# Attention front of a one-core transformer layer: six output slots for values, the first queries and keys in halves, plain scores one tile sooner

## The chip, the cores and the metric

The kernel runs on one core of a Trainium2 chip. The metric is device time in microseconds (us). The engines are TensorE (PE in the profile, its weight loads PEld), VectorE (DVE), ScalarE (ACT), GpSimd (POOL) and SyncE (SP), which here issues all DMA transfers on one queue.

## What is computed

A layer on 2048 tokens of width 512: a normalisation, causal attention with 16 heads of 32, and a gated feed-forward part with a hidden width of 4096.

```python
xn = layernorm(x)
qkv = xn @ w_qkv.T                       # 3 x 16 heads x 32
scores = q @ k.T / sqrt(32)              # causal: only keys up to the query
attn = softmax(scores) @ v
gate, up = xn @ Wg.T, xn @ Wu.T
out = x + attn @ w_o.T + (gelu(gate) * up) @ Wd.T
```

All of it is float32; the kernel splits an operand in a high and a low part and multiplies in three passes where one pass is too coarse.

## The kernel before

Three blocks follow each other: `norm_and_project`, `attention`, `project_and_feed_forward`. Within a block each engine runs its own list of instructions, in the order in which the program issues them, and waits on semaphores; there is no planner.

`norm_and_project` makes the normalised tokens and the queries and keys, which it stores to `qk_scratch` in memory, and the values of the first two tiles of 128 tokens (`V_FIRST`), left in PSUM in `p_v`.

`attention` begins with the *value stage*. TensorE makes the values of tiles 2 to 15, twelve matmuls each (`values`, lines 49 to 51 in `mm3`), in turn in three PSUM banks, `bank_st` (`p_v` twice and `p_st3`, `ST_BUFS` = 3). It makes tile v when ScalarE has placed tile v - 3. ScalarE's `value_out(v)` (lines 727 to 735) waits for the tile, waits for the slot, copies the tile to one of two slots in `o_sb` (line 731), and copies its heads of the first two pairs to `v_stack` (line 733). SP then stores the slot to `v_scratch` in memory (line 540).

```python
            if v >= 2:
                act.wait_ge(v_stored[v % 2], 16 * (v // 2))
```

The attention goes by eight pairs of heads. A pair needs its queries and keys in `q_stack` and `k_stack`: `load_head` (lines 517 to 523) issues six DMAs of 32 rows by 2048 columns, 256 KB each, for each of its two heads. SP's order in the value stage is: head 0 of pair 0, store 0, head 1, stores 1 to 8, head 0 of pair 1, stores 9 and 10, head 1 of pair 1, stores 11 to 15.

*Units* are plain score tiles (queries in rows), at most 512 keys wide, `scores(n)`, line 855; VectorE takes their row maxima, with a mask on the diagonal (line 767) or without (line 771). They use four banks `p_s` in turn, so unit n waits for the maximum of unit n - 4 (`bank_free`). A pair has 80 units. 44 of pair 0 are put behind value tiles 6 to 14: four behind tile 6, five behind each other (`BEHIND_V`, `FIRST_V`). The LEAD stage behind tile 15 has the next eight units and the first eight *transposed scores* (`scores_t`, line 883), whose exps ScalarE makes (line 708) and GpSimd sums (line 635). Then the main loop runs 80 groups: a group has eight transposed scores, its units, four products with the values (line 909) and row sums (line 923). The units run ahead of what needs them by a fixed number: `unit_end` says how many are done after each group, 12 in the first, then 8 in each until all 640 are made. The row maxima are split by GpSimd (lines 650 to 658) and turned into rows by TensorE (line 865).

On the first use of a pair (units 0 and 1) TensorE waits for `qk_loaded`. Later pairs are loaded by SP in the middle of the pair before.

Of the kernel before, what the change touches and what calls it, by code (L numbers as in the profile page):

```python
# [20 lines left out]
F32 = mybir.dt.float32  # L21
# [5 lines left out]
ACT = mybir.ActivationFunctionType  # L27
# [3 lines left out]
S = 2048  # L31
H = 512
NH = 16
D = H // NH
MLP = 4096
KT = H // P
TT = S // P
W = 512
TC = S // W
# [272 lines left out]
def attention(nc, qk_scratch, v_scratch, sum_scratch, rsum_scratch, wo_t, wo_sb, attn_t, xn_hi, xn_lo, e_sb, wv_hi, wv_lo, p_v,  # L312
# [5 lines left out]
    PB = 2  # L318
# [10 lines left out]
    UNITS_FIRST = (20, 12)  # L329
    UNITS_AHEAD = 56  # L330
    TURN_LEAD = 1


    STEPS = [(qc, kt, max(0, kt * P - qc * W)) for qc in range(TC) for kt in range(4 * qc + 4)]
# [11 lines left out]
    NU = len(UNITS)  # L346
    UNITS_TO = [sum(1 for a, i, b, w in UNITS if i < 4 * r + 4) for r in range(TC)]
    NUNIT = PAIRS * NU
    MASKED_UNITS = [n for n in range(NUNIT) if UNITS[n % NU][2] == UNITS[n % NU][1] // 4]

    BEHIND_V = {v: 4 if v == 6 else 5 for v in range(6, TT - 1)}
    FIRST_V = sum(BEHIND_V.values())
    FIRST = FIRST_V + LEAD * 2
    unit_end, done = [], FIRST
# [58 lines left out]
    with ExitStack() as ctx:  # L415
# [3 lines left out]
        def sem(name):  # L419
            return ctx.enter_context(nc.semaphore(name))  # L420

        q_stack = [[sb(f"q_stack{i}{a}", [P, S], F32R) for a in range(2)] for i in range(PB)]
        k_stack = [[sb(f"k_stack{i}{a}", [P, S], F32R) for a in range(2)] for i in range(PB)]
# [4 lines left out]
        o_sb = sb("o_sb", [P, 2, 2, HALF], F32)  # L428
        rsum_rows = sb("rsum_rows", [P, S], F32)
# [15 lines left out]
        p_o = ctx.enter_context(nc.psum_tensor("p_o", [P, 2, HALF], F32))  # L445

        v_out = sem("v_out")
        v_stored = [sem(f"v_stored{i}") for i in range(2)]
        v_placed = [sem(f"v_placed{i}") for i in range(PB)]
        consts = sem("consts")  # L450
        filled = sem("filled")
        o_cleared = sem("o_cleared")
        qk_loaded = [[sem(f"qk_loaded{i}{a}") for a in range(2)] for i in range(PB)]
        v_loaded = [sem(f"v_loaded{i}") for i in range(PB)]
        scored = sem("scored")
        maxed = sem("maxed")
# [26 lines left out]
        def bank_st(x):  # L483
            return p_v[:, x % ST_BUFS, :] if x % ST_BUFS < V_FIRST else p_st3[:, :]
# [25 lines left out]
        def pooled_to(k, i):  # L510
            return max(count for j in range(i + 1) for vector, count in [made[k, j]] if not vector)

        def attn_rows(p, a, qc):
            cols = slice((p // 2) * S + qc * W, (p // 2) * S + (qc + 1) * W)
            return attn_t[(2 * (p % 2) + a) * D:(2 * (p % 2) + a + 1) * D, cols]

        def load_head(sp, p, a):
            rows = slice((2 * p + a) * D, (2 * p + a + 1) * D)
            for strip, (q_part, k_part) in enumerate(((0, 0), (0, 1), (1, 0))):
                to = slice(strip * D, (strip + 1) * D)  # L520
                sp.dma_start(q_stack[p % PB][a][to, :].bitcast(F32),
                             qk_scratch[0, q_part, rows, :]).then_inc(qk_loaded[p % PB][a], 16)
                sp.dma_start(k_stack[p % PB][a][to, :].bitcast(F32),
                             qk_scratch[1, k_part, rows, :]).then_inc(qk_loaded[p % PB][a], 16)

        def load_v(sp, p):
            sp.dma_start(v_stack[p % PB][:, :, :, :],
# [2 lines left out]

        @block.sync
        def _(sp):
            load_head(sp, 0, 0)
            for v in range(TT):
                if v == 1:
                    load_head(sp, 0, 1)
                if v in (9, 11):
                    load_head(sp, 1, v // 11)
                sp.wait_ge(v_out, v + 1)
                sp.dma_start(v_scratch[v * P:(v + 1) * P, :, :],  # L540
                             o_sb[:, v % 2, :, :].rearrange("p b (h d) -> p (b h) d", d=D)).then_inc(v_stored[v % 2], 16)
            sp.dma_start(wo_sb[:, :, :], wo_t.rearrange("(k p) o -> p k o", p=P)).then_inc(wo_loaded, 16)

            def store_chunk(p, qc):
                c = p * TC + qc
                sp.wait_ge(o_copied, c + 1)
                for a in range(2):
                    for h in range(2):
                        rows = (2 * a + h) * D
                        sp.dma_start(attn_rows(p, a, qc)[:, h * HALF:(h + 1) * HALF],  # L550
                                     o_sb[rows:rows + D, c % 2, 0, :]).then_inc(o_stored[c % 2], 16)
                        first = qc * W + h * HALF
                        sp.dma_start(sum_scratch[2 * p + a:2 * p + a + 1, first:first + HALF],
                                     o_sb[rows:rows + 1, c % 2, 1, :]).then_inc(o_stored[c % 2], 16)

            def load_sums(p):
                for stored in o_stored:
                    sp.wait_ge(stored, 128 * (p + 1) * (TC // 2))
                if p:
                    sp.wait_ge(sums_inverted, p)  # L560
                sp.dma_start(compact[:, :], sum_scratch[2 * p:2 * p + 2, :].rearrange("h (a b) -> (h a) b", b=2 * S // P)
                             ).then_inc(sums_loaded, 16)

            def load_reciprocals(p):
                sp.wait_ge(sums_inverted, p + 1)
                sp.dma_start(rsum_scratch[2 * p:2 * p + 2, :].rearrange("h (a b) -> (h a) b", b=2 * S // P),
                             rcompact[:, :]).then_inc(rsums_out, 16)
                sp.wait_ge(rsums_out, 16 * (p + 1))
                if p >= 2:
                    sp.wait_ge(normalised, TC * (p - 1))  # L570
                for a in range(2):
                    rows = (2 * (p % 2) + a) * D
                    sp.dma_start(rsum_rows[rows:rows + D, :],
                                 rsum_scratch[2 * p + a, :].partition_broadcast(D)).then_inc(rows_loaded, 16)

            for p in range(PAIRS):
                if 0 < p < PAIRS - 1:
                    sp.wait_ge(st_ready, p * NS * PIECES)
                    for a in range(2):
                        load_head(sp, p + 1, a)  # L580
                    sp.wait_ge(pv_done, p * NS)
                    for stored in v_stored:
                        sp.wait_ge(stored, 16 * (TT // 2))
                    load_v(sp, p + 1)
                if p > 0:
                    store_chunk(p - 1, TC - 1)
                    load_sums(p - 1)
                if p < PAIRS - 1:
                    store_chunk(p, 0)
                if p > 0:  # L590
                    load_reciprocals(p - 1)
                if p < PAIRS - 1:
                    for qc in range(1, TC - 1):
                        store_chunk(p, qc)
            sp.wait_ge(wo_loaded, 16)
# [91 lines left out]
        def _(act):  # L687
# [23 lines left out]
            def copy_out(p, qc):  # L711
                c = p * TC + qc
                act.wait_ge(rows_done, (p * NS + CHUNK_START[qc]) // GS + qc + 1)
                if c < 2:
                    act.wait_ge(v_stored[c], 16 * (TT // 2))
                elif p == PAIRS - 1 and qc == 2:
                    act.wait_ge(divided, 4)
                else:
                    act.wait_ge(o_stored[c % 2], 128 * (c // 2))
                nc.scalar.activation(o_sb[:, c % 2, :, :], p_o[:, :, :], ACT.Copy).then_inc(o_copied, 1)  # L720
# [5 lines left out]

            def value_out(v):
                act.wait_ge(v_projected, v + 1)
                if v >= 2:
                    act.wait_ge(v_stored[v % 2], 16 * (v // 2))  # L730
                nc.scalar.activation(o_sb[:, v % 2, :, :].rearrange("p b w -> p (b w)"), bank_st(v), ACT.Copy).then_inc(v_out, 1)
                for i in range(PB):
                    nc.scalar.activation(v_stack[i][:, v, :, :],
                                         bank_st(v)[:, 2 * i * D:2 * (i + 1) * D].rearrange("p (a d) -> p a d", a=2),
                                         ACT.Copy).then_inc(v_placed[i], 1)
# [19 lines left out]
        def _(dve):  # L755
# [30 lines left out]
            def divide(qc):  # L786
# [5 lines left out]
                else:  # L792
                    dve.wait_ge(o_copied, c + 1)
                    o = o_sb[:, c % 2, :, :]
                dve.wait_ge(maxed, NUNIT)
                if qc:
# [42 lines left out]
        def _(pe):  # L839
# [8 lines left out]
            def scores(n):  # L848

                p, u = divmod(n, NU)  # L850
                a, i, b, w = UNITS[u]
                if u < 2:
                    pe.wait_ge(qk_loaded[p % PB][a], 96 * (p // PB + 1))
                bank_free(slot[n])
                nc.tensor.matmul(p_s[:, slot[n] % S_BUFS, 0:w], q_stack[p % PB][a][0:ROWS, i * P:(i + 1) * P],  # L855
                                 k_stack[p % PB][a][0:ROWS, b * W:b * W + w], start=True, stop=True
                                 ).then_inc(scored, 1)
# [572 lines left out]
```

## Time and profile before

| | us |
|---|---|
| median of 3 runs | 1840.53 |
| lowest, highest | 1839.3, 1840.86 |
| profiled execution | 1840.19 |
| its span | 1838.4 |

In the page, a group of instructions is named by line, engine and tile. In a timeline, the numbers in front are the start and the length; in brackets stands the idle time of the engine before the instruction and what ended it. Matmuls overlap: one of 512 columns is listed with 0.39 us, and the next starts 0.23 us later at the full clock, so paces are read from starts. Many small neighbours are merged into one row with their count.

### The profile page before, as it was taken

How to read it: one execution, taken by the hardware profiler on the slowest of the kernel's cores; microseconds unless marked ns; L12 is line 12 of the kernel's file. 1: busy time of each engine (PE TensorE's matmuls, PEld its weight loads, DVE VectorE, ACT ScalarE, POOL GpSimd, SP SyncE). 2: the span in 40 equal slices, each digit the busy share in tenths (PEclk: the TensorE clock that was granted, in tenths of full speed). 3: DMA queues.
4: the chain of work that ended last, by engine and by line, in shares of the span. 5: the costliest groups of instructions: out<-in, count | busy, mean ns of one | idle time of the engine just before them, and what ended most of it. 6: DMA issues, size and time to landing. Idle time of an engine off the chain costs nothing.

```text
span 1838.4 us, 28874 instructions
## 1 busy us (share of the span) xinstructions
PE 1796.9 (98%) x10496; PEld 1348.4 (73%) x10496; DVE 1127.0 (61%) x1724; ACT 702.3 (38%) x1151; POOL 721.6 (39%) x720
## 2 busy tenths in 40 slices
PE   7989999999999998999999999999999999999998
PEld 6877666666666654478888888888888888888887
DVE  5416666666666666457665675666566567566654
ACT  3323666666666664023232332232232323323322
POOL 1431778778778774021222222222222222222221
PEclk9999999999999998999999999999999999999999
DMA  8675043143143100521101101100110110110002
GB/s 286 218 215 151 10 102 73 37 102 73 37 102 72 38 17 21 197 69 35 35 0 34 34 0 34 34 26 9 34 34 0 34 34 3 31 34 0 1 1 92
DMA packets 73105, 108.59 MB, mean 59 GB/s; under 512 B 24704, under 2 KB 44784, under 8 KB 69360
## 3 DMA queue, kind: packets, MB, share of 16 engines
q1 hardware_dynamic: 73008, 107.34, 21.2%
q8 instruction: 56, 0.92, 0.2%
q14 instruction: 41, 0.34, 0.1%
HBM read 74.04 MB, written 29.59 MB: 56 GB/s over the span
## 4 chain that ended last, share of the span: by engine, by line
PE 60%; DVE 0%; issue 0%
PE p_up L51 6%; PE p_gate L51 6%; PE p_gate L49 6%; PE p_up L49 6%; PE p_gate L50 6%; PE p_up L50 6%; PE p_out L51 6%; PE p_out L49 6%; PE p_out L50 6%; PE p_out L1358 1%; PE p_gate L1358 1%; PE p_up L1358 1%; DVE acc L1288 0%
## 5 line engine op out<-in xcount | busy, mean ns | idle before, releaser
L1200 POOL TENSOR_SCALAR poly<-poly 128x1024 f32<-128x1024 f32 (+1 forms) x65 | 71.4, 1098 | 841.3 <-ACT poly L1162 841.3
L635 POOL TENSOR_TENSOR e_sum<-e_sb 128x512 f32<-128x512 f32 (+1 forms) x244 | 291.2, 1220 | 99.2 <-PE p_o L923 89.8
L771 DVE TENSOR_REDUCE max_part<-p_s 128x1 f32<-128x512 f32 x384 | 241.2, 683 | 51.5 <-PE p_s L855 50.2
L708 ACT ACTIVATE e_sb<-p_v 128x512 f32<-128x512 f32 (+3 forms) x427 | 216.5, 552 | 129.7 <-PE p_v L883 70.2
L1263 DVE SCALAR_TENSOR_TENSOR inter<-inter,gate 128x1024 f32<-128x1024 f32 (+1 forms) x65 | 78.6, 1209 | 248.4 <-ACT inter L1168 247.6
L855 PE MATMUL p_s<-k_stack,q_stack 96*128 96x512 f32 (+3 forms) x640 | 217.2, 393 | 0.7 <-DVE max_part L771 0.5
L767 DVE CUSTOM_DVE_ANT_0 recip<-p_s,score_mask 128x128 bf16<-128x128 f32 (+3 forms) x256 | 119.7, 486 | 156.0 <-PE p_s L855 153.9
L1161 ACT ACTIVATE gate<-p_gate 128x1024 f32<-128x1024 f32 (+1 forms) x65 | 66.0, 1015 | 354.6 <-PE p_gate L51 354.6
L49 PE MATMUL p_gate<-xn_hi,w_hi 128*128 128x512 f32 x512 | 199.6, 390 | 0.0
L50 PE MATMUL p_gate<-xn_lo,w_hi 128*128 128x512 f32 x512 | 199.2, 389 | 0.0
L51 PE MATMUL p_gate<-xn_hi,w_lo 128*128 128x512 f32 x512 | 199.2, 389 | 0.0
L49 PE MATMUL p_up<-xn_hi,w_hi 128*128 128x512 f32 x512 | 199.2, 389 | 0.0
L50 PE MATMUL p_up<-xn_lo,w_hi 128*128 128x512 f32 x512 | 199.2, 389 | 0.0
L51 PE MATMUL p_up<-xn_hi,w_lo 128*128 128x512 f32 x512 | 199.2, 389 | 0.0
L49 PE MATMUL p_out<-i_hi,w_hi 128*128 128x512 f32 x504 | 196.1, 389 | 0.0
L50 PE MATMUL p_out<-i_lo,w_hi 128*128 128x512 f32 x504 | 196.1, 389 | 0.0
L51 PE MATMUL p_out<-i_hi,w_lo 128*128 128x512 f32 x504 | 196.1, 389 | 0.0
L1203 POOL TENSOR_TENSOR poly<-poly,gate 128x1024 f32<-128x1024 f32 (+1 forms) x65 | 177.8, 2735 | 5.4
L883 PE MATMUL p_v<-q_stack,k_stack 128*128 128x512 f32 (+3 forms) x427 | 159.2, 397 | 8.1 <-ACT e_sb L708 5.1
L855 PEld LDWEIGHTS p_s<-k_stack,q_stack 96*128 96x128 f32 x640 | 115.3, 189 | 47.0 <-issue 28.5
L909 PE MATMUL p_o<-e_sb,v_stack 128*32 128x256 f32 (+1 forms) x2304 | 148.6, 372 | 0.0
L1283 DVE TENSOR_TENSOR acc<-acc,p_out 128x2048 f32<-128x2048 f32 x63 | 143.6, 2280 | 3.3 <-PE p_out L51 3.3
(146 smaller groups left out, 3090.6 us busy)
## 6 DMA issues: line engine op xcount, KB each, us to landing
q_stack<-qk_scratch SPq DMA_DIRECT2D x48, 256.0 KB, 6.5
k_stack<-qk_scratch SPq DMA_DIRECT2D x48, 256.0 KB, 7.2
qk_scratch<-out_hi SPq DMA_DIRECT2D x32, 256.0 KB, 2.6
qk_scratch<-out_lo SPq DMA_DIRECT2D x32, 256.0 KB, 3.3
scales<-in_gate_up_s SPq DMA_DIRECT2D x128, 64.0 KB, 2.3
xn_lo_scratch<-xn_lo SPq DMA_DIRECT2D x4, 1024.0 KB, 5.2
v_scratch<-o_sb SPq DMA_DIRECT2D x16, 256.0 KB, 2.6
xn_lo<-xn_lo_scratch SPq DMA_DIRECT2D x1, 4096.0 KB, 16.7
```

The source lines that it names most:

```text
L49: nc.tensor.matmul(out, w_hi, x_hi, start=first, stop=False)
L50: nc.tensor.matmul(out, w_hi, x_lo, start=False, stop=False)
L51: return nc.tensor.matmul(out, w_lo, x_hi, start=False, stop=last)
L635: nc.gpsimd.tensor_tensor(*operands(k, i), ALU.add).then_inc(pool_summed, 1)
L708: nc.scalar.activation(e_sb[:, x % E_BUFS, 0:w], bank_st(x)[:, 0:w], ACT.Exp, scale=SCALE).then_inc(exp_done, 1)
L767: nc.vector.tensor_tensor_reduce(out=masked_scores[:, m % 2, 0:w], in0=p_s[:, slot[n] % S_BUFS, 0:w], in1=score_mask[:, W - w:], scale=1.0 ...
L771: nc.vector.reduce_max(part, p_s[:, slot[n] % S_BUFS, 0:w], AX.X).then_inc(maxed, 1)
L855: nc.tensor.matmul(p_s[:, slot[n] % S_BUFS, 0:w], q_stack[p % PB][a][0:ROWS, i * P:(i + 1) * P], k_stack[p % PB][a][0:ROWS, b * W:b * W + ...
L883: last = nc.tensor.matmul(bank_st(x)[:, 0:W - q0], k_stack[p % PB][a][:, kt * P:(kt + 1) * P], q_stack[p % PB][a][:, qc * W + q0:(qc + 1) ...
L909: last = nc.tensor.matmul(p_o[(2 * a + h) * D:(2 * a + h + 1) * D, 0, first - h * HALF:], v_stack[p % PB][:, kt, a, :], e_sb[:, (g * PIECE ...
L1203: nc.gpsimd.tensor_tensor(part_of(poly, h, parts), part_of(poly, h, parts), part_of(gate, h, parts), ALU.mult).then_inc(poly_done, 1)
L1283: nc.vector.tensor_tensor(here, here, p_out[:, :, :], ALU.add).then_inc(added, 1)
```

## The change

1. The values on their way to memory have six slots (`V_SLOTS`), not two: four in `rsum_rows`, which nothing uses until pair 1, and two in `o_sb`. `value_out(v)` waits for a store from tile 6 on, for that of tile v - 6. The waits of `copy_out` and of SP's `load_v` count the stores of the new slots.
2. The queries and keys of pair 0 are loaded in two halves of 1024 columns. SP issues the first half of both heads (twelve DMAs of 128 KB, semaphores `first_loaded`), stores 0 and 1, the second half of both (twelve more), and stores 2 to 8; the rest of its order stays. Units 0 and 1 wait for the first half, units 24 and 25, which are the first to read beyond column 1023, for the second.
3. `BEHIND_V` has five units behind each of the value tiles 5 to 14: 50 and not 44. By the rule of `unit_end` the first group then has 8 units and not 12, the later ones 8 as before and two units further ahead, and the last group with units has 6.

```diff
+    V_SLOTS = 6
+    FIRST_COLS = S // 2
+    SECOND = UNITS_TO[FIRST_COLS // W - 1]
-    BEHIND_V = {v: 4 if v == 6 else 5 for v in range(6, TT - 1)}
+    BEHIND_V = {v: 5 for v in range(5, TT - 1)}
...
-        v_stored = [sem(f"v_stored{i}") for i in range(2)]
+        v_stored = [sem(f"v_stored{i}") for i in range(V_SLOTS)]
+        first_loaded = [sem(f"first_loaded{a}") for a in range(2)]
...
+        def v_slot(v):
+            slot_v = v % V_SLOTS
+            return rsum_rows[:, slot_v * W:(slot_v + 1) * W] if slot_v < TC else \
+                o_sb[:, slot_v - TC, :, :].rearrange("p b w -> p (b w)")
+
+        def v_stores(slot_v):
+            return 16 * len(range(slot_v, TT, V_SLOTS))
...
-        def load_head(sp, p, a):
+        def load_head(sp, p, a, cols=slice(0, S), loaded=None):
+            loaded = loaded or qk_loaded[p % PB][a]
...
-                sp.dma_start(q_stack[p % PB][a][to, :].bitcast(F32),
-                             qk_scratch[0, q_part, rows, :]).then_inc(qk_loaded[p % PB][a], 16)
+                sp.dma_start(q_stack[p % PB][a][to, cols].bitcast(F32),
+                             qk_scratch[0, q_part, rows, cols]).then_inc(loaded, 16)
...
-            load_head(sp, 0, 0)
+            for a in range(2):
+                load_head(sp, 0, a, slice(0, FIRST_COLS), first_loaded[a])
             for v in range(TT):
-                if v == 1:
-                    load_head(sp, 0, 1)
+                if v == 2:
+                    for a in range(2):
+                        load_head(sp, 0, a, slice(FIRST_COLS, S))
...
                 sp.dma_start(v_scratch[v * P:(v + 1) * P, :, :],
-                             o_sb[:, v % 2, :, :].rearrange("p b (h d) -> p (b h) d", d=D)).then_inc(v_stored[v % 2], 16)
+                             v_slot(v).rearrange("p (h d) -> p h d", d=D)).then_inc(v_stored[v % V_SLOTS], 16)
...
-                    for stored in v_stored:
-                        sp.wait_ge(stored, 16 * (TT // 2))
+                    for slot_v in range(V_SLOTS):
+                        sp.wait_ge(v_stored[slot_v], v_stores(slot_v))
...
-                    act.wait_ge(v_stored[c], 16 * (TT // 2))
+                    act.wait_ge(v_stored[TC + c], v_stores(TC + c))
...
-                if v >= 2:
-                    act.wait_ge(v_stored[v % 2], 16 * (v // 2))
-                nc.scalar.activation(o_sb[:, v % 2, :, :].rearrange("p b w -> p (b w)"), bank_st(v), ACT.Copy).then_inc(v_out, 1)
+                if v >= V_SLOTS:
+                    act.wait_ge(v_stored[v % V_SLOTS], 16 * (v // V_SLOTS))
+                nc.scalar.activation(v_slot(v), bank_st(v), ACT.Copy).then_inc(v_out, 1)
...
-                if u < 2:
+                if p == 0 and u < 2:
+                    pe.wait_ge(first_loaded[a], 96)
+                elif u < 2 if p else u in (SECOND, SECOND + 1):
                     pe.wait_ge(qk_loaded[p % PB][a], 96 * (p // PB + 1))
```

## Rows read from the trace of the kernel before

**Rows 1.** The page, its first part: TensorE's busy time and share.

```profile
PE 1796.9 (98%) x10496; PEld 1348.4 (73%) x10496; DVE 1127.0 (61%) x1724; ACT 702.3 (38%) x1151; POOL 721.6 (39%) x720
```

**Rows 2.** Table of stages: start:end length, busy per engine, granted clock, DMA share, GB/s.

```profile
125.00:126.00 1.00, 0.00 (x0) 0.00 (x0) 0.00 (x0) 0.00 (x0) 0.94 (x2) 0.96 1.10 231
132.00:133.00 1.00, 0.47 (x2) 0.00 (x0) 0.00 (x0) 0.00 (x0) 0.70 (x1) 0.62 0.45 170
```

**Rows 3.** Timeline of TensorE, value tiles 4 to 6 (start, length, operation).

```profile
120.73 0.39 PE L49 MATMUL p_v<-wv_hi,xn_hi 128*128 128x512 f32 x1
...
123.22 0.39 PE L51 MATMUL p_v<-wv_hi,xn_lo 128*128 128x512 f32 x1
126.98 0.79 PE L49 MATMUL p_st<-wv_hi,xn_hi 128*128 128x512 f32 x1 [3.37 <-ACT v_stack L733]
...
131.84 0.63 PE L51 MATMUL p_st<-wv_hi,xn_lo 128*128 128x512 f32 x1
134.22 0.50 PE L49 MATMUL p_v<-wv_hi,xn_hi 128*128 128x512 f32 x1 [1.75 <-ACT v_stack L733]
```

**Rows 4.** Timeline of ScalarE, its two long waits in the value stage.

```profile
126.10 0.60 ACT L731 ACTIVATE o_sb<-p_st 128x512 f32<-128x512 f32 x1 [9.41 <-DMA v_scratch<-o_sb]
...
133.34 0.60 ACT L731 ACTIVATE o_sb<-p_v 128x512 f32<-128x512 f32 x1 [6.41 <-DMA v_scratch<-o_sb]
```

**Rows 5.** Timeline of SP's queue: first and sixth load of head 0, store 1.

```profile
115.13 0.34 SPq L521 DMA_DIRECT2D q_stack<-qk_scratch  x1
...
118.31 0.42 SPq L523 DMA_DIRECT2D k_stack<-qk_scratch  x1
...
122.06 23.44 SPq L540 DMA_DIRECT2D v_scratch<-o_sb  x8
```

**Rows 6.** Issue to landing, by tile: issued at 115.13, at 118.31, at 122.06.

```profile
DMA to landing us min/median/max: 3.8/3.8/3.8
...
DMA to landing us min/median/max: 7.0/7.0/7.0
...
DMA to landing us min/median/max: 11.2/11.2/11.2
```

**Rows 7.** Timelines of TensorE and VectorE: units behind tile 6, five units behind tile 11.

```profile
137.06 0.63 PE L855 MATMUL p_s<-k_stack,q_stack 96*128 96x128 f32 x4
...
137.44 0.29 DVE L767 CUSTOM_DVE_ANT_0 recip<-p_s,score_mask 128x128 bf16<-128x128 f32 x1 [21.64 <-PE p_s L855]
...
156.54 1.51 PE L855 MATMUL p_s<-k_stack,q_stack 96*128 96x512 f32 x5
157.89 0.45 PE L49 MATMUL p_v<-wv_hi,xn_hi 128*128 128x512 f32 x1
```

**Rows 8.** Timelines: LEAD stage's table load, first group, a late full group.

```profile
174.87 1.28 ACT L708 ACT_TABLE_LOAD   x1
...
179.21 0.47 PE L883 MATMUL p_st<-q_stack,k_stack 128*128 128x512 f32 x1
...
184.31 1.29 PE L909 MATMUL p_o<-e_sb,v_stack 128*32 128x256 f32 x18
...
182.29 3.67 DVE L771 TENSOR_REDUCE max_part<-p_s 128x1 f32<-128x512 f32 x6
...
675.51 0.40 PE L883 MATMUL p_st<-q_stack,k_stack 128*128 128x512 f32 x1
...
679.25 1.07 PE L923 MATMUL p_o<-e_sum,ones 128*32 128x256 f32 x16
```

**Rows 9.** Timelines of SP's queue and TensorE: pair 2's last load and first units.

```profile
244.08 0.42 SPq L523 DMA_DIRECT2D k_stack<-qk_scratch  x1
...
269.46 0.33 PE L855 MATMUL p_s<-k_stack,q_stack 96*128 96x128 f32 x2
```

**Rows 10.** Table of stages late in the attention; TensorE's timeline at the last stage.

```profile
692.00:696.00 4.00, 4.00 (x39) 2.01 (x43) 1.29 (x2) 1.74 (x5) 1.22 (x1) 0.57 0.00 0
...
731.16 9.96 PE L1358 MATMUL p_gate<-acc,wo_sb 128*128 128x512 f32 x16 [4.24 <-PEq L415]
```

More of the change, by code:

```diff
@@ L520, in load_head @@
                 to = slice(strip * D, (strip + 1) * D)
-                sp.dma_start(q_stack[p % PB][a][to, :].bitcast(F32),
-                             qk_scratch[0, q_part, rows, :]).then_inc(qk_loaded[p % PB][a], 16)
-                sp.dma_start(k_stack[p % PB][a][to, :].bitcast(F32),
-                             qk_scratch[1, k_part, rows, :]).then_inc(qk_loaded[p % PB][a], 16)
+                sp.dma_start(q_stack[p % PB][a][to, cols].bitcast(F32),
+                             qk_scratch[0, q_part, rows, cols]).then_inc(loaded, 16)
+                sp.dma_start(k_stack[p % PB][a][to, cols].bitcast(F32),
+                             qk_scratch[1, k_part, rows, cols]).then_inc(loaded, 16)
         def load_v(sp, p):
```

## The prediction

> **What bounds the kernel now.** I read the page first: TensorE is busy 98% of the span [rows 1], so the kernel can only get shorter where TensorE idles or runs slow, or where it has less to do. The change touches the front of the attention, so the second view is the 1 us table of stages: the granted clock leaves its full level (2.4 GHz) for the half (1.2 GHz) at 125.9 us and is back at 132.8 (worked out from the means of the two edge microseconds, 0.96 and 0.62) [rows 2]. Third, TensorE's timeline. Value tile 4 is twelve matmuls from 120.73 to a last start at 123.22, 0.227 us apart, so a tile takes 2.72 us. Tile 5 should start at 123.45 and starts at 126.98, after 3.37 us idle; its last matmul starts at 131.84, so its twelve are 0.43 us apart at the half clock; tile 6 starts only at 134.22, after another 1.75 us idle [rows 3]. Both releasers are ScalarE's copies of a tile three earlier, and ScalarE's timeline says why these are late: it idles 9.41 us and 6.41 us until a store to v_scratch has landed [rows 4]. Those stores sit on SP's queue behind the loads of the first pair's queries and keys: six loads of 256 KB from 115.13, then store 0, six more, store 1 at 122.06 [rows 5]. The first load lands 3.8 us after its issue (118.9), the sixth 7.0 us after (125.3), store 1 11.2 us after (133.3) [rows 6]. Loads of this kind land 1.28 us apart ((125.3 - 118.9)/5). So DMA traffic holds two output buffers, these hold ScalarE, ScalarE holds three PSUM banks, and these hold TensorE.
>
> **The change, part by part.** *Six slots for values on their way.* value_out(v) waits for a store only from v = 6, and then for the store six tiles earlier. Tiles 0 to 5 leave as soon as TensorE has made them. Tile 5 starts at 123.45, ends at 126.17, with the full clock. Before, tile 6 began at 134.22 and its first matmul gap was 0.34 instead of 0.23. Removed: 134.22 - 126.17 + 0.11 = **8.16 us**: 3.53 and 1.95 of idle between matmuls, 2.57 (12 matmuls at 0.441 rather than 0.227) of half clock, and the small rest.
>
> Is something else late next? Bytes are the same: 12 loads and two stores landed by 133.3 [rows 6], and stores 2 to 5 add 1.0 MB at the loads' pace at most (4 x 1.28 = 5.1 us), so by 138.4. A tile with five units takes 2.72 + 1.35 = 4.07 [rows 7], so value 8 is due at 126.2 + 1.4 + 2 x 4.07 + 2.72 = 138.4 and wants store 2, the first of these four (134.6 at worst); value 9, due 142.5, wants store 3. Tiles 8 and 9 also have two further tiles of cover in PSUM before TensorE would feel them. I put this at nothing; without that cover each microsecond of wait would cost one.
>
> *Halves.* SP issues the first 1024 columns of both heads as twelve loads of 128 KB, then stores 0 and 1, then the other twelve. An issue takes 0.53 us ((122.06 - 115.13)/13) [rows 5], so the twelfth is issued at about 121.0. The twelve carry the bytes of the old head 0 and by bytes land at 125.3; by issue, 121.0 + 3.8 = 124.8. The first plain score of head 0 is due at 126.2, of head 1 at 126.4: covered by 1.0 us. If the smaller packets cost more, TensorE waits for the difference. I take 0, and 0 to 2 us for the range. The second halves are issued by 129 (26 issues), and land by about 134; they are wanted by unit 24, the last of the five behind tile 9, near 143: eight microseconds of cover. SP's waits for v_out 3 and later stand behind these twelve issues (6.4 us), which delays stores 2 to 5 to 129 and later; they have six slots now, so nobody waits.
>
> *Plain scores one tile sooner.* Tiles 5 to 14 now carry five units each, 50 for 44 before. The six more are 512 wide, 6 x 0.227 = 1.36 us. One more switch between values and units: five units with about 2560 columns (1.14 us at 0.227 per 512) took from 156.54 to 157.89, so 0.2 us over [rows 7]. Behind tile 5 the fifth unit needs the bank of the first: TensorE began the four after tile 6 at 137.06, VectorE read the first at 137.44 for 0.29 [rows 7], so unit 4 can start some 0.8 us after unit 0, 0.3 us late. VectorE's maxima now run beside GpSimd's fills of k_stack; no row shows the two together, VectorE has no others for 21 us before, so 0 to 0.3, taken 0. Added in the value stage: **1.9 us** (1.6 to 2.4).
>
> That work is taken out later. FIRST goes from 52 to 58, the first group of the main loop has 8 units and not 12, and all later groups have 8 as before, until the last one with units has 6 and not 8. The LEAD stage keeps eight units, and there ScalarE sets the pace (1.28 us for its table, then the exps) [rows 8], so their widths don't matter. The first group takes TensorE from 179.21 to 184.31 up to its products [rows 8]: 5.10 us for eight transposed scores, eight units of 512 columns and two of 128, some 16.5 x 0.227 = 3.7 of own work; VectorE's maxima, 3.67/6 = 0.61 us each, come one after another there [rows 8]. After, it is eight transposed scores and seven units worth six of 512: 14 x 0.227 = 3.2. The saving lies between 0.5 (own work alone) and 1.9 (no waiting left). The nearest row is a full group of eight scores and seven units late in the attention, 675.51 to 679.25, 3.74 us [rows 8]: 5.10 - 3.74 = **1.4 us**. The piece behind the products is 512 columns before and after. The last group: 0 to 0.45 (two of 0.227), taken 0.1, since from there on ScalarE paces the loop.
>
> Being two units ahead also makes the first two units of every pair come two places earlier, still behind their loads: pair 2's last load is issued at 244.08 and, even at 11.2 us, lands at 255.3; its first units run at 269.46 [rows 9], and would be some 4 us sooner. Covered.
>
> *The rest* (wait for two semaphores more per pair on SP, other slot names, ScalarE's writes to rsum_rows instead of o_sb in the same shape) costs nothing measurable: all of it lies on engines that wait anyway.
>
> Sum: -8.16 + 1.9 - 1.4 - 0.1 = **-7.76 us**. The profiled execution took 1840.19 for a span of 1838.4; 1832.4 after. The median is 0.34 above it: **1832.8**. Its own range, with 1.6 to 2.4 added and 0.5 to 2.35 saved, is 1831.6 to 1834.5.
>
> **Rivals.** *The clock falls elsewhere (A).* The same kernel is at the half clock at 692 to 696 (mean 0.57), where TensorE is busy but in small pieces, and when it begins the last stage at 731.16 after 4.24 us idle [rows 10]. All of this now comes 8 us earlier, and the stage from 174 to 184 has gaps of the same kind at full clock. A further half-clock stretch like that at 692 (about 3.4 us by its mean, (1 - 0.57) x 4 / 0.5) costs up to half its length, 1.7 us; two cost 3.4: 1834.5 to 1836.2. The same can go the other way, one or two fewer: 1829.4 to 1831.1. For it: the stretches are short and near an edge. Against: the three runs lie within 1.6 us of each other. The Trainium skill (TensorE: Matmul & The Clock Gate, Part 1) says that the number of slow matmuls after a gap varies from run to run since the monitor runs free of the program; it would make this rival likelier, and no single trace here can show it.
>
> *Halved loads cost like whole ones (B), the case on the other side.* It is one place: unit 1 behind tile 5, which needs the twelfth half. At 1.28 us apart that lands at 118.9 + 11 x 1.28 = 133.0, against 126.4 due: 6.6 us idle, and then a tile at half clock, 2.6 us as now. -8.16 + 6.6 + 2.6 + 1.9 - 1.5 = +1.4: **1842.0**. It starts to cost above 0.68 us per half ((126.4 - 118.9)/11), and eats the whole gain at some 1.15. By bytes a half is 0.64, so the margin is thin but the loss small at first; SP's spacing of 0.53 speaks against a large one. The Trainium skill (DMA: Bandwidth & Descriptors, Anatomy of one DMA) speaks against halving: a fixed 2.0 us per transfer, so by its fit an estimated 2.3 us for a half and 2.6 for a whole; were landings spaced in that ratio, 1.13 us, this would give 1840.3. Against it as a spacing: whole loads land 1.28 us apart here [rows 6], less than the fixed part alone, so transfers overlap.
>
> *Half loads a little late, or the six moved units not given back (C).* 1 to 2 us idle at unit 1 with the clock kept, or 1.4 not saved, or both: 1833.8 to 1836.2.
>
> *It doesn't do what it says (D).* A slot or a wait still ties ScalarE to the traffic in the same place, and one of the two stalls stays: the second, 1.95 us, or the first with its half clock, 6.1: 1834.8 to 1838.9.
>
> **How the numbers follow.** Forecast 0.56; A slower 0.14, A faster 0.10; B 0.03; C 0.13; D 0.04. Predicted 1832.8. From 1830.2 (most of A faster) to 1836.4 (A slower, C) no more than 0.15 is left out. A measurement of this kernel can tell some 0.2% (3.7 us) from no change: faster is below 1836.8, which holds the forecast, both A and C, 0.93; within 0.2%: D and most of B, 0.05; slower (above 1844.2) if B were worse than priced or D came with it, 0.02.
>
> **What would show it.** Value tiles 2 to 6 in TensorE's timeline 2.72 us apart with no idle; no wait of ScalarE on v_scratch; granted clock 1.00 from 120 to 170; units at 126.2 directly behind tile 5; the LEAD stage 6.3 us earlier than now (8.16 - 1.9); the first group in 3.7 us up to its products and not 5.1. Wrong: a wait of TensorE at 126 us on q_stack or k_stack (B, C), or a half-clock stretch between 165 and 185 or a longer one near 690 to 735 (A).

## Result, and the profile after

Measured in turns on one chip, the changed kernel takes 1833.81 us (median of six executions, 1832.85 to 1836.19), the kernel before 1840.64 (six, 1839.3 to 1842.04). The ratio is 0.9964, 95% interval 0.9952 to 0.9976: 6.8 us less (4.4 to 8.8 by the interval), where 7.8 were forecast. So the total can't tell the two apart, and what follows goes by stages. The profiled execution of the changed kernel is the slowest of its six (1836.19), so the profiled pair shows only 4.0 us, and the medians must not be explained by the difference of the two spans alone.

The page of the changed kernel, its first part (busy time of the engines):

```profile
span 1834.4 us, 28896 instructions
...
PE 1798.6 (98%) x10496; PEld 1345.9 (73%) x10496; DVE 1129.7 (62%) x1724; ACT 702.4 (38%) x1151; POOL 721.5 (39%) x720
```

Against [rows 1] TensorE is recorded as 1.7 us busier in a span 4 us shorter. The table of stages of the changed kernel, at the two edges that [rows 2] showed:

```profile
125.00:126.00 1.00, 1.00 (x6) 0.82 (x5) 0.00 (x0) 0.00 (x0) 0.94 (x2) 1.00 1.08 289
132.00:133.00 1.00, 1.00 (x6) 0.80 (x5) 1.00 (x3) 0.00 (x0) 0.85 (x3) 1.00 1.03 393
```

The clock is 1.00 in both, where it was 0.96 and 0.62, and TensorE fills both. Its timeline, against [rows 3] and [rows 8]:

```profile
123.29 0.39 PE L49 MATMUL p_st<-wv_hi,xn_hi 128*128 128x512 f32 x1
...
125.78 0.39 PE L51 MATMUL p_st<-wv_hi,xn_lo 128*128 128x512 f32 x1
126.01 1.18 PE L874 MATMUL p_s<-k_stack,q_stack 96*128 96x128 f32 x5
127.03 0.40 PE L49 MATMUL p_v<-wv_hi,xn_hi 128*128 128x512 f32 x1
...
172.86 0.47 PE L902 MATMUL p_st<-q_stack,k_stack 128*128 128x512 f32 x1
...
176.91 1.29 PE L928 MATMUL p_o<-e_sb,v_stack 128*32 128x256 f32 x18
```

Tile 5 runs from 123.29 to 126.01 at 0.227 a matmul, five plain scores follow at once, tile 6 starts at 127.03 and not at 134.22. ScalarE, which waited 9.41 and 6.41 us for stores [rows 4], waits for none; its row for tile 5:

```profile
126.21 0.60 ACT L748 ACTIVATE o_sb<-p_st 128x512 f32<-128x512 f32 x1 [1.89 <-PE p_st L51]
```

SP's queue, the twelfth half load of the changed kernel and, from the view by tile, its landing, against [rows 5] and [rows 6]:

```profile
114.99 0.34 SPq L536 DMA_DIRECT2D q_stack<-qk_scratch  x1
...
121.07 0.42 SPq L538 DMA_DIRECT2D k_stack<-qk_scratch  x1
```

```profile
DMA to landing us min/median/max: 3.6/3.6/3.6
```

It lands at 121.07 + 3.6 = 124.7, 1.3 us before the first plain score.

**Where the time went.** Four marks are easy to find in each trace: SP's first load of the attention, the first product (L909 or L928) of the first group, and the turns of the maxima (64-column matmuls with ident_bf, L865 or L884) in pair 1 and, the same turn, in pair 7. Six pairs lie between the last two. Rows of TensorE's timeline, first before, then after:

```profile
245.21 0.41 PE L865 MATMUL p_s<-ident_bf,max_cols 128*64 128x128 bf16 x4
...
658.99 0.30 PE L865 MATMUL p_s<-ident_bf,max_cols 128*64 128x128 bf16 x2
```

```profile
238.03 0.41 PE L884 MATMUL p_s<-ident_bf,max_cols 128*64 128x128 bf16 x4
...
653.90 0.30 PE L884 MATMUL p_s<-ident_bf,max_cols 128*64 128x128 bf16 x2
```

| us | first load | load to product | product to turn in pair 1 | six pairs | pair 7's turn to end | span |
|---|---|---|---|---|---|---|
| before | 115.13 | 69.18 | 60.90 | 413.78 | 1179.4 | 1838.4 |
| after | 114.99 | 61.92 | 61.12 | 415.87 | 1180.5 | 1834.4 |
| difference | -0.1 | **-7.3** | +0.2 | **+2.1** | +1.1 | -4.0 |

The front gave what was forecast for it, almost. Two things were not in the sum: the pairs each take 0.35 us longer (2.09/6), and the rest after pair 7's turn is 1.1 us longer in this execution. The two further units ahead reach some four groups into that rest; Rival A below comes back to it.

### The profile page after: what moved, and what is told of

Same layout as the page of the kernel before. It is cut to its first block, busy times and chain, and to the rows that moved or that the text cites. A ratio compares the mean times of both kernels' runs of the same rounds, so it can differ in the third digit from the quotient of the medians.

```text
span 1834.4 us, 28896 instructions
## 1 busy us (share of the span) xinstructions
PE 1798.6 (98%) x10496; PEld 1345.9 (73%) x10496; DVE 1129.7 (62%) x1724; ACT 702.4 (38%) x1151; POOL 721.5 (39%) x720
## 4 chain that ended last, share of the span: by engine, by line
PE 60%; DVE 0%; issue 0%
PE p_up L51 6%; PE p_gate L51 6%; PE p_gate L49 6%; PE p_up L49 6%; PE p_up L50 6%; PE p_gate L50 6%; PE p_out L51 6%; PE p_out L49 6%; PE p_out L50 6%; PE p_out L1377 1%; PE p_gate L1377 1%; PE p_up L1377 1%; DVE acc L1307 0%
## 5 line engine op out<-in xcount | busy, mean ns | idle before, releaser
L788 DVE TENSOR_REDUCE max_part<-p_s 128x1 f32<-128x512 f32 x384 | 248.1, 685 | 146.0 <-PE p_s L874 145.6
L928 PE MATMUL p_o<-e_sb,v_stack 128*32 128x256 f32 (+1 forms) x2304 | 149.6, 374 | 0.0
```

The lines of the kernel that those rows point to most:

```text
L788: nc.vector.reduce_max(part, p_s[:, slot[n] % S_BUFS, 0:w], AX.X).then_inc(maxed, 1)
L928: last = nc.tensor.matmul(p_o[(2 * a + h) * D:(2 * a + h + 1) * D, 0, first - h * HALF:], v_stack[p % PB][:, kt, a, :], e_sb[:, (g * PIECE ...
```

## Experiments

"Pairs" below is always the time between the two turns, against 413.78 before; "front" the time from first load to first product, against 69.18. The first theory for the pairs: the plain scores come in groups of eight, wide and narrow ones at fixed places; two units further on, other widths come to stand where nothing else covers them.

**Groups aligned again (e1).** All of the change, but a first group of six units, so that 58 + 6 = 64 are done after it, as 52 + 12 were before.

```diff
-        done = min(NUNIT, max(done + UNITS_GROUP, min(
+        done = min(NUNIT, max(done + (UNITS_GROUP if k else 6), min(
```

> The changed kernel, with the first group of the main loop cut from 8 units to 6, so that all later groups hold the same units as in the kernel before (64 done after the first group, not 66). In the profile of the changed kernel the turn of the maxima stands 7.34 us before that of the kernel before at 184 us, and only 5.27 us before it at 646 us: 2.1 us are lost over seven pairs, about 0.3 us in each. Theory T: it is the place of the narrow units. With two units more ahead, the eighth unit of a group, which runs alone behind the products, is a wide one (512 columns) where it was a narrow one (128 to 384), and the narrow ones fall where TensorE waits for the exps anyway. By T this kernel keeps the 7.3 us to the end of the attention and takes 1833.8 - 2.1 - 0.3 = 1831.4 us. Rival R: the loss comes from the front of the change (slots, loads) or from the stage being shorter: no change, 1833.8 us.

Measured 1831.44 (1830.14 to 1832.05), ratio to the kernel before 0.9945 [0.9931, 0.9958]. Pairs 413.63: the loss is gone. Front 61.40.

**Nothing moved (e2).** Slots and halves, with the old order of plain scores.

```diff
-    BEHIND_V = {v: 5 for v in range(5, TT - 1)}
+    BEHIND_V = {v: 4 if v == 6 else 5 for v in range(6, TT - 1)}
```

> The changed kernel with the old number of units behind the value tiles (44, from tile 6 on), six slots and halves kept. By theory T it has the whole 8.1 us of the stalls and neither the 1.95 us added in the value stage, nor the 1.05 us saved in the first group, nor the 2.1 us lost in the pairs: 1840.6 - 8.1 = 1832.5 us, so 1 us under the changed kernel and 1 above the aligned one. Rival: the six units moved are worth what the first group saves and nothing is lost later: 1834 to 1835 us.

Measured 1831.36 (1830.33 to 1832.16), 0.9946 [0.9933, 0.996]. Pairs 413.70, front 60.96. TensorE's timeline of this kernel, start of the first group and its first product:

```profile
171.38 0.47 PE L902 MATMUL p_st<-q_stack,k_stack 128*128 128x512 f32 x1
...
176.47 0.85 PE L928 MATMUL p_o<-e_sb,v_stack 128*32 128x256 f32 x12
```

The first load was issued at 115.51, so the first group starts 55.87 behind it, before 64.08 (179.21 - 115.13): the stalls were worth 8.21. In the changed kernel it is 57.87: the six units added 2.00. Up to its products the first group takes 5.09 here, 5.10 before, 4.05 in the changed kernel: moving them took 1.05 out. So moving them loses 0.95 in the front and 2.1 in the pairs; even aligned (e1) it wins nothing over this kernel.

**Only the shift, on the kernel before (e3).** Two units further on in the main loop, stalls and all.

```diff
-    UNITS_AHEAD = 56
+    UNITS_AHEAD = 58
```

> The kernel before, with one constant changed: units are two further ahead (58 and not 56), so the first group has 14 units and all later ones hold the same units as in the changed kernel. Nothing at the front is touched. Theory T: slower by the 2.1 us that the changed kernel loses over the pairs, plus up to 0.5 us in the first group: 1842.7 to 1843.2 us, with 0.3 us lost in each pair of the trace. Rival R: the kernel before, 1840.6 us.

Measured 1846.44 (1843.93 to 1849.53), 1.0025 [1.0016, 1.0034]. Pairs 415.89, the same +2.1 as in the changed kernel, with none of its other edits: the shift alone does it. In its round the kernel before took 1841.39, so it is 5.1 us slower, where 2.1 to 2.6 were expected. The profiled execution, its slowest, has a front of 73.13, 3.95 more than before, with 2.72 us idle at tile 6 and the half clock behind it. TensorE's timeline:

```profile
135.89 0.79 PE L49 MATMUL p_v<-wv_hi,xn_hi 128*128 128x512 f32 x1 [2.72 <-ACT v_stack L733]
```

The longer idle costs nothing: tile 6 starts 19.1 us behind the first load here (135.89 - 116.81) as before (134.22 - 115.13), since ScalarE waits for the same store, until 18.2 us behind that load in both; only tile 5 was done sooner, since the full clock came back in its middle. What costs is a second stretch of half clock, from 135.3 to 142.1 us, and the 14 units of the first group: it starts 66.96 us behind the first load (64.08 before) and takes 6.17 us up to its products (5.10), together the 3.95. How many of the other executions have that stretch isn't known.

**Slots alone (e4).** The changed kernel's six slots with whole loads in their old order and no unit moved.

```diff
-            for a in range(2):
-                load_head(sp, 0, a, slice(0, FIRST_COLS), first_loaded[a])
+            load_head(sp, 0, 0)
...
-                if v == 2:
-                    for a in range(2):
-                        load_head(sp, 0, a, slice(FIRST_COLS, S))
+                if v == 1:
+                    load_head(sp, 0, 1)
...
```

> The kernel before with the six slots alone: whole loads in the old order, 44 units from tile 6 on. Tiles 2 to 6 run without a gap and end at 128.9 us. Then unit 1 wants all of head 1, which landed at 132.7 us in the kernel before. Theory: 3.8 us idle there, and the clock may fall as it did (up to 2.6 us more): 1840.6 - 8.1 + 3.8 to 6.4 = 1836.3 to 1838.9 us, so the halves are worth as much as they hide. Rival: the stores were all that was late, the loads are not: 1832.5 us.

Measured 1838.23 (1836.94 to 1839.46), 0.9985 [0.9976, 0.9994]. Front 66.50, 2.7 less. TensorE's timeline behind tile 6:

```profile
129.13 0.22 PE L870 MATMUL p_s<-k_stack,q_stack 96*128 96x128 f32 x1
133.15 1.01 PE L870 MATMUL p_s<-k_stack,q_stack 96*128 96x128 f32 x3 [3.79 <-DMA k_stack<-qk_scratch]
133.95 0.63 PE L49 MATMUL p_v<-wv_hi,xn_hi 128*128 128x512 f32 x1
```

The stall has another name: the second plain score needs head 1, whose whole loads land last. The half clock (0.63 a matmul) comes with it.

**Halves alone (e5).** The kernel before with the loads halved; two slots, no unit moved.

```diff
-            load_head(sp, 0, 0)
+            for a in range(2):
+                load_head(sp, 0, a, slice(0, FIRST_COLS), first_loaded[a])
...
-                if v == 1:
-                    load_head(sp, 0, 1)
+                if v == 2:
+                    for a in range(2):
+                        load_head(sp, 0, a, slice(FIRST_COLS, S))
...
```

> The kernel before with the halved loads alone, two slots, 44 units from tile 6 on. Store 0 now stands behind twelve half loads, as many bytes as before, and lands near 125.5 us, so the first stall of 3.5 us and the half clock after it stay. Store 1 lands about 126 us and not 133.3, so the second stall (1.95 us) goes. Store 2 stands behind the twelve second halves (near 133 us) and may hold value 4 and so tile 7 by up to a microsecond. Expected: the kernel before less 1 to 2 us, 1839 to 1840.5 us with the kernel before at 1841. The rival says that the halves are worth what slots alone missed (5 us): 1836 us.

Measured 1837.25 (1834.84 to 1839.48), 0.9979 [0.9969, 0.9989], some 2 us better than expected. TensorE's timeline:

```profile
126.92 0.79 PE L49 MATMUL p_st<-wv_hi,xn_hi 128*128 128x512 f32 x1 [3.13 <-ACT v_stack L739]
...
132.21 0.63 PE L49 MATMUL p_v<-wv_hi,xn_hi 128*128 128x512 f32 x1
```

The first stall and the half clock stay (3.13 us for 3.37), the second stall goes (tile 6 at 132.21). Front 67.17, -2.0, as expected. This execution is the fastest of its ten; the rest of its gain lies behind the pairs: 1176.1 there, with a clock of 1.00 where the kernel before has 0.92. The table of stages, 46 us near the attention's end, first before, then this kernel:

```profile
685.00:731.00 46.00, 38.62 (x375) 19.64 (x374) 30.62 (x34) 22.36 (x49) 23.47 (x21) 0.92 0.01 1
```

```profile
681.00:727.00 46.00, 37.25 (x380) 19.10 (x378) 32.27 (x39) 24.36 (x52) 24.64 (x23) 1.00 0.01 1
```

**Eight more units ahead (e6), a shift by four (e7), the first groups levelled (e8).**

```diff
-    UNITS_AHEAD = 56
+    UNITS_AHEAD = 64
```

> The changed kernel with its units further ahead still, eight more than in the aligned one: the first group has 14, the later ones hold the units of the kernel before, one group earlier. It tells being ahead from being off the grid. If the loss of 0.35 us per pair comes from which unit stands alone behind the products, there is none here: the lag between the turns at 191 and 673 us stays within 0.2 us, and the time is the aligned kernel's 1831.4 us plus up to 1.8 us for eight more units before the last groups. If running ahead costs by itself, the loss is 0.35 us per pair or more and the time is 1834 us or above.

Measured 1840.22 (1838.99 to 1843.28), 0.9997 [0.9988, 1.0007]: 7 us and more above the first branch of the expectation; the second, that running ahead costs by itself, holds. The alignment is the good one, but pairs are 419.63, 6.0 more than in e1, and with 14 units in the first group the front is 64.34, 2.9 more. Together they are the 8.8 us between the medians. The waits of TensorE from 200 to 640 us (us in total, times, longest), first this kernel, then e1:

```profile
PE p_o L942 <- POOL e_sum L652: 8.9, 6, 1.5
```

```profile
PE p_o L942 <- POOL e_sum L652: 2.9, 6, 0.5
```

TensorE now waits up to 1.5 us, once a pair, for GpSimd's sums, 6.0 us more in all, as much as the pairs are longer than in e1 (419.63 - 413.63). Running further ahead is not free. GpSimd's timeline shows what stands in the way: the row maxima of a block are complete sooner, and their five short operations (lines 667 to 675, 350.33 to 351.7 us) run ahead of the sums that TensorE waits for, where in e1 they run behind them (353.09).

```diff
-        done = min(NUNIT, max(done + UNITS_GROUP, min(done + UNITS_FIRST[min(k, 1)], UNITS_GROUP * (k + 1) + UNITS_AHEAD)))
+        done = min(NUNIT, done + (UNITS_GROUP if k else 10))
```

> The changed kernel with a first group of 10 units, so every later group is four units further than in the aligned one. The units alone behind the products have 4096 columns in a pair, as in the kernel before (the changed kernel has 4608), but they are other units. If only their width counts, the pair takes what it took before, within 0.13 us, and the kernel 1831.4 to 1832.4 us. If any shift off the old grid costs, 0.3 us or more are lost per pair, as in the changed kernel: 1833.5 us or more.

Measured 1834.31 (1833.1 to 1836.27), 0.9962 [0.9947, 0.9976]. The expectation left out that the first group has four units more than in e1: its front is 62.62, 1.22 more. Pairs 414.72, +0.16 a pair, where equal widths behind the products promised none. The theory in its first form, which counts only these, is not complete.

```diff
-    UNITS_FIRST = (20, 12)
+    UNITS_FIRST = (10, 12)
```

(e8, with nothing moved as in e2.)

> Slots and halves, 44 units behind the value tiles, and the first two groups of the main loop with 10 units each and not 12 and 8. The first group of 12 takes 5.10 us up to its products for 3.7 us of own work, since the maxima set the pace. With 10 it should take 4.4 to 4.7 us and the second some 0.3 more. Expected 0 to 0.5 us under the variant with slots, halves and 12 units (1831.36 us): 1830.9 to 1831.4 us. Rival: the second group has no slack for VectorE either, no change or slower.

Measured 1831.08 (1830.33 to 1831.18), 0.9942 [0.9926, 0.9959]. Front 60.04, 0.9 less than e2; 0.4 of it is lost again within the pairs (414.11). No difference from e2 that the times can tell.

**Which place is exposed (e9, e10).** In a group of eight, the eighth unit runs behind the products. The first theory named this place alone: behind the products only the next group's scores follow. Here the eighth unit runs ahead of the products too, in e9 in the aligned kernel, in e10 in the changed one.

```diff
-        ring += units[:7 * len(units) // 8] + TURNS[k] + units[7 * len(units) // 8:]
+        ring += units + TURNS[k]
...
-                        for part in {0: (0, 1, 2), 2: (3,), 4: (4, 5), 6: (6,)}[n]:
+                        for part in {0: (0, 1, 2), 2: (3,), 4: (4, 5), 6: (6, 7)}[n]:
...
-                some_units(7, 8)
```

> The aligned kernel (first group of 6) with no unit behind the products: all eight of a group go between the transposed scores. Together with the next run it tests the place itself. If the unit behind the products is 0.1 to 0.23 us that nothing hides, while those between the scores are partly hidden by ScalarE's pace, this saves up to 0.18 us a group, 12 us over 72 groups: 1820 to 1831 us. If that unit covers a wait for the exps after the products, it costs: above 1831.4 us, with more waits of TensorE on the exps.

> The changed kernel with no unit behind the products. By the theory that the unit alone behind the products makes the 0.35 us lost per pair (0.22 of it by widths), this one and the run before it differ per pair by 0.13 us at most in the turns from 238 to 652 us. If the loss is anywhere else in the group, they differ by 0.35 us as before.

e9: 1833.76 (1831.96 to 1834.89), 0.9962 [0.9947, 0.9976], pairs 415.31. e10: 1837.0 (1835.28 to 1838.46), 0.998 [0.997, 0.9989], pairs 416.95. The shift still costs 1.64 over six pairs, 0.27 a pair, with nothing behind the products. The theory in this form falls: the place behind the products isn't needed for the loss. How much of the 0.35 comes from there in the changed kernel these two can't say, since the moved eighth unit may be just as exposed where it stands now. They also show that the eighth unit stands well where it was (e9 loses 0.28 a pair to e1).

What the two traces show ahead of the products, at the turn in pair 1, first e1, then the changed kernel:

```profile
237.82 0.31 PE L874 MATMUL p_s<-k_stack,q_stack 96*128 96x128 f32 x1
238.05 0.41 PE L884 MATMUL p_s<-ident_bf,max_cols 128*64 128x128 bf16 x4
...
241.34 0.33 PE L874 MATMUL p_s<-k_stack,q_stack 96*128 96x128 f32 x1
241.50 0.45 PE L902 MATMUL p_v<-q_stack,k_stack 128*128 128x512 f32 x1
```

```profile
237.62 0.47 PE L874 MATMUL p_s<-k_stack,q_stack 96*128 96x512 f32 x1
238.03 0.41 PE L884 MATMUL p_s<-ident_bf,max_cols 128*64 128x128 bf16 x4
...
241.31 0.50 PE L874 MATMUL p_s<-k_stack,q_stack 96*128 96x512 f32 x1
241.65 0.40 PE L902 MATMUL p_v<-q_stack,k_stack 128*128 128x512 f32 x1
```

A narrow unit is there in e1, a wide one in the changed kernel, in both places: 0.23 against 0.41 up to the turn, 0.16 against 0.34 up to the next score. The reading, which no run isolates: units inside the group run while ScalarE's exps set the pace of the transposed scores; these two don't. So the second form of the theory: two places are exposed, the last unit ahead of the products and the one behind them. By the list of units, a pair puts 8192 columns into them when aligned, 9216 when shifted by two. At 0.227 us for 512 columns the 1024 more are worth 0.45 us, of which 0.35 was measured. But e7 has 8192 in the two places as well, so this form doesn't explain its 0.16 either.

**Four slots (e11).** e2 with four slots, which leaves o_sb out of the value stage, and ScalarE's wait for the stores from o_sb with it.

```diff
-    V_SLOTS = 6
+    V_SLOTS = 4
...
-                    act.wait_ge(v_stored[TC + c], v_stores(TC + c))
+                    pass
```

> Slots and halves with 44 units behind the value tiles, and four slots instead of six. Value 4 wants store 0 (lands near 125.5 us) while due at 123.5, and value 6 wants store 2 (lands near 133 us) while due at 129: ScalarE waits 2 and 4 us, but the tiles that need their banks, 7 and 9, come at 130 and 137.5 us. Expected: as with six slots, 1831.4 us, with ScalarE's waits on v_scratch in the trace and no wait of TensorE on v_stack before the last tile. Rival: the waits reach TensorE, 1832.5 us or more.

Measured 1831.43 (1830.61 to 1832.28), 0.9953 [0.9936, 0.9969], front 60.93: the same as six. ScalarE waits for stores again, two times and 10.2 us in all, and TensorE feels none of it. ScalarE's waits from 110 to 175, then TensorE's from 100 to 200:

```profile
ACT rsum_rows L748 <- DMA v_scratch<-rsum_rows: 10.2, 2, 6.3
```

```profile
PE p_v L902 <- ACT v_stack L750: 0.5, 1, 0.5
```

**Narrow ones last (e12).** A forecast of the second form: e2, with the eight units of each group sorted so that the narrow ones stand in the exposed places. That takes a pair's columns in them from 8192 to 5376.

```diff
+    UNITS = [u for g in range(0, len(UNITS), 8) for u in sorted(UNITS[g:g + 8], key=lambda u: -u[3])]
```

> Six slots, halves and 44 units behind the value tiles (1831.36 us), and within every eight units of a pair the wide ones first and the narrow ones last; nothing else. The two runs before say that the unit behind the products makes only 0.10 of the 0.375 us lost per pair, and the trace of the group at 231 to 238 us shows where the rest lies: after the last transposed score of a diagonal group one more unit follows ahead of the turn, 0.41 us for a wide one and 0.23 for a narrow one, while what stands between the scores hides behind the exps. So by the theory in its second form two places of a group are bare, its seventh and its eighth unit. The changed kernel has 1024 columns more there per pair than the aligned one, for 0.375 us. This order takes 1408 columns out of each of the two places, 2816 per pair, so about 1.0 us per pair and up to 8 us in all: 1823 to 1828 us. Rival: between the scores a wide unit costs what it saves at the end, and TensorE's total of work decides: 1831.4 us.

Measured **1827.78** (1825.61 to 1829.61), 0.9927 [0.9914, 0.9941], the best of all: 13.2 us below the kernel before (1841.0 in its round), 3.6 below e2. Pairs 410.24, so 0.59 a pair less (413.78 - 410.24 = 3.54 over six); the front is 61.58, 0.6 more than e2's. By columns alone it would be 2816 x 0.227/512 = 1.25 a pair. The direction holds, and the size is about half.

The program and the traces say where the other half may be. In six of a pair's ten groups a transposed score still follows the seventh unit; only in the four whose transposed scores cross the diagonal does it stand last ahead of the products. Counting the seventh in those four alone, a pair puts 5376 columns into exposed places when aligned, 6656 in the changed kernel, 6016 in e7 and 3712 in e12. By columns that is +0.57, +0.28 and -0.74 us, measured +0.35, +0.16 and -0.59: the order of all three comes out, which neither form above gives, the sizes at 0.6 to 0.8. The times from one group's first matmul into p_o to the next one's, means over five pairs, agree where one width alone changes: where only an eighth unit widens by 256 columns, 6.62 us in e1 and 6.73 in the changed kernel (by columns 0.11 more); where only a seventh of a diagonal group widens by 384, 7.35 and 7.52 (0.17 more). But one such time falls by 0.13 (7.95 to 7.83) where neither width changes, so the order inside a group counts too. This count was made after the runs, and none was built to test it.

## Why the prediction was right, and where it wasn't

- **Six slots, halves: -8.16.** Right: 8.21 (e2). Both stalls and the half clock are gone. Neither edit does it alone (-2.7 and -2.0 in the front), together they give more than the sum of these: with slots alone the wait moves to head 1's loads, with halves alone the buffers still hold ScalarE for the first store. The prediction costed the two together and neither by itself.
- **Halves in time.** Right: due 126.0, landed 124.7 (forecast 124.8 to 125.3). Rival B would have shown 6.6 us idle there; there is none. The Trainium skill (DMA: Bandwidth & Descriptors, Anatomy of one DMA) gives a fixed cost per transfer, measured there for transfers that GpSimd issues, where SP issues these, which the prediction didn't say. The twelve halves took 9.7 us from first issue to last landing (124.7 - 115.0) and the six whole loads 10.2 (125.3 - 115.1), so the trace doesn't show it as a cost of halving. The second halves landed by 132.7 (127.85 + 4.8; forecast 134).
- **Six units in the value stage: +1.9.** 2.00.
- **First group: -1.4.** 1.05 (5.10 to 4.05), inside the 0.5 to 1.9 given.
- **"All later groups have 8 as before": priced at nothing. This step failed.** Eight units per group, but not the same eight, and each pair pays 0.35 us. The prediction looked at the piece behind the products for the first group alone, and never walked the pattern through a pair. e1 takes the loss away with one number, e3 makes it in the kernel before, so the shift is shown as the cause. That it acts through the widths in the exposed places is borne out by e12 in its direction; how much each place costs is argued.
- **Rival C** ("the six moved units not given back", 1833.8 to 1836.2) is where the time came out, at its lower edge, but for another reason than it names: half of what they cost (1.05 of 2.00) is given back in the first group, and what is lost is lost in the pairs. The time lies in the range of the prediction's own sum as well, whose upper end works out to 1834.3 (1840.53 - 8.16 + 2.4 - 0.5) and not 1834.5.
- **Rival A.** No half clock between 165 and 185. Near the attention's end there are two such stretches in the changed kernel's profiled execution (681.6 to 685.1 and 702.1 to 705.5), as in the one of before (692.5 to 696 and 719.9 to 723.3); e1, e2, e6 and e8 have one, e5 and e7 none. From the last turn of the maxima to the last stage's first matmul (p_gate) it is 36.8 us at the full clock (e5, e7, e12), 37.7 with a stretch at 710 (e1, e2, e8), and 38.2 in the changed kernel with its second: 0.9 and 1.4 us each, where the prediction gave up to 1.7. The 1.1 us behind pair 7's turn looks like the same thing: the changed kernel and e3 both take 35.0 us from that turn to the last one, with a stretch inside, e1 and e2 33.3 and e10, which has the shift too, 33.2, all without; no execution of the changed kernel without the stretch was profiled. The six executions of the changed kernel have mean clocks from 0.996 to 0.999, and the profiled one is among the lowest. The Trainium skill (TensorE: Matmul & The Clock Gate, Part 1) says that the number of slow matmuls at a kernel's start differs from run to run; the prediction carried this over to gaps, and of these the runs show that the mean clock differs between executions of one kernel.
- **The sum.** Front -7.3, pairs +2.1, as profiled: -5.2, and the medians differ by 6.8 (by the interval of the ratio 4.4 to 8.8). For e2 it is -8.3 against 9.9 (7.4 to 12.3). Both medians show some 1.6 us more than the stages, which both intervals allow. Part of it may be the clock behind pair 7, which profiles of single executions can't settle. So that the predicted 1832.8 came so close to 1833.8 is luck in part: the 2.1 us that it missed, and 0.35 too much for the first group, were partly met by something not forecast either.

## What to carry over

When work that runs ahead of a loop is shifted by a part of a group, count which items now stand where nothing covers them, through a whole period; "the same number per group" says nothing if the items differ. Put narrow items in exposed places and wide ones beside paced work: here that one sort was worth 3.6 us (e12 against e2). Free buffers and the order of loads belong together: cost each edit alone, since the wait may only change its name.

## What the runs showed of the hardware

- Halving 256 KB loads into 128 KB ones (rows of 4 KB in place of 8) cost nothing: the same bytes landed within 9.7 us of the first issue and within 10.2. Of the first twelve halves each landed 2.7 to 3.7 us after its issue, of the second twelve, behind two stores, 3.9 to 4.8; the first whole load took 3.8 [rows 6].
- Half-clock stretches come and go between the profiled kernels in the thin end of the attention, where TensorE works in small pieces (38.6 us busy of 46 before), at 0.9 to 1.4 us each in the part from the last turn to the last stage.
- How much of ScalarE's wait TensorE feels depends on what else TensorE has ready: ScalarE's 6.41 us cost TensorE 1.75 before [rows 3, 4], where no plain scores had begun, and its 6.3 us in e11, with plain scores behind the tiles, nothing.
